# The opening of a Perceiver layer: loads on two queues in order of use, half of the tokens prepared after the first energies

## The chip, the cores and the metric

The kernel runs on one core of a Trainium2 chip. The metric is the device time of one launch in microseconds (us), lower is better. Engines are named as in the profile: PE (TensorE, with PEld for its weight loads), DVE (VectorE), ACT (ScalarE), POOL (GpSimd) and SP (SyncE, which in this kernel only issues DMAs). A trailing q, as in SPq, is an engine's instruction queue.

## The reference

One layer of a Perceiver on x (32 batches of 32 tokens, 256 wide) and a context of 257 rows per batch, cut to its steps:

```python
h = layernorm(x)                       # 1024 tokens
Q = h @ Wq.T + bq                      # 16 heads of 16
K, V = ctx @ Wk.T + bk, ctx @ Wv.T + bv
e = where(mask == 0, -1e20, Q K^T / 4); x = x + softmax(e) V @ Wo.T + bo
x = x + causal_self_attention_with_rope(layernorm(x))
x = x + top2_mixture_of_8_experts(layernorm(x))   # gelu(x w0) * (x w1) @ wo
```

All products of float32 data are made of three TensorE products of rounded halves: a value is split into a high part (an ACT copy that rounds) and a low part (DVE: value minus high part), and hi*lo + lo*hi + hi*hi is accumulated (`product3`). So each weight or activation that enters such a product costs a transpose on PE, an ACT copy and a DVE subtraction.

## The kernel before

The program has three stages: an opening ("prelude") that loads x and three weights and makes all queries; 32 steps of cross attention, one per batch b, arranged as 8 groups j of 4 (u = 0 to 3), into which the self attention of earlier groups is woven; and routing and expert products. Each engine has its own hand-written list of instructions; semaphores (`wait_ge`) are the only order between engines.

The prelude is a list `slots`: `bias` (biases turned), `w` 0 to 2 (Wq, Wk, Wv turned and split), `lastT` (the last context row of each batch), `kl` and `vl` (its key and value), `xT` 0 to 3 (256 normed tokens each, turned and split), `q` 0 to 3 (queries: two halves of the features, two halves of the tokens). PE works through it in that order, ACT keeps the high part, and DVE the low part. All of it has to be over (`first_act` and `first_dve` at their full counts) before `turn_ctx(0)` begins the cross attention: context 0 turned, `keys(0)`, `values(0)`, context 1 turned, and then step 0 with `energies(0)`.

In a step b the engines do, in this order: PE `energies(b)`, `turn_ctx(b+2)`, `keys(b+1)`, `outputs(b-2)`, `turn_probs(b-1)`, `values(b+1)`; ACT four exponentials with the split of context b+2 among them, then `keep_keys(b+1)` and `keep_values(b+1)`; DVE the four `maxima`, and so on; POOL spreads the queries (`spread`) and scales the probabilities. In group 0 five more weights are turned, at the end of each step (`late_weights`: weights 3 and 4 in step 0, 5 and 6 in step 1, 7 in step 2).

All loads are issued by SP, in one list. Weights in `BY_HEAD` (0, 1, 4, 5: Wq, Wk and the self attention's W_Q, W_K) are loaded with their rows rearranged, in two DMAs each of 128 KB. The zero fills of `V`, `PTd` and `Vm` are the first work of DVE; POOL adds the bias bo to x (`xbo_done`) before step 0.

```python
pe.wait_ge(sm["first_act"], NS)          # after all 15 slots
pe.wait_ge(sm["first_dve"], sum(by_dve))
turn_ctx(0, 0, 16); keys(0, 0); values(0, 0); turn_ctx(1, 1, 16)
```

## Time and profile before

| | |
|---|---|
| time, median of 3 runs | 563.48 us (563.48, 567.03, 556.87) |
| the profiled execution | 566.69 us, span 564.8 us |
| busy, share of the span | PE 501.6 us (89%), DVE 406.2 (72%), ACT 325.1 (58%), POOL 247.3 (44%) |
| PE busy from 0 to 10 us | none |
| PE busy from 10 to 20 us | 3.34 us |
| DMA | 48.91 MB, mean 87 GB/s |

The span runs from the first to the last instruction; 1.9 us of the profiled execution lie around it. Times in the trace count from the span's start. A matmul is pipelined, so its cost in a row of them is the distance between two starts, not its own duration. PEclk is the granted clock of TensorE, where 1.00 is 2.4 GHz and 0.50 is 1.2 GHz.

### The profile page before, as it was taken

The numbers are of one execution on the slowest core, as the hardware profiler recorded it, in microseconds if no ns is written. First come the engines' busy times: TensorE is split into PE (matmuls) and PEld (weight loads), VectorE is DVE, ScalarE is ACT, GpSimd is POOL, SyncE is SP. The second block draws the span as 40 slices with busy tenths as digits, with TensorE's granted clock in tenths as the row PEclk, the third lists the DMA queues.
The fourth block names the chain that finished last, engine by engine and source line by source line (L and its number), as shares of the span: only waits on it lengthen the run. The fifth ranks groups of instructions, "written<-read, shape, count | busy, mean of one in ns | idle before, by whom it ended". The sixth has DMA issues, their size and how long they took to land.

```text
span 564.8 us, 18262 instructions
## 1 busy us (share of the span) xinstructions
PE 501.6 (89%) x6637; PEld 460.1 (81%) x6637; DVE 406.2 (72%) x1005; ACT 325.1 (58%) x839; POOL 247.3 (44%) x337
## 2 busy tenths in 40 slices
PE   0777999989999999999976657899999999999996
PEld 0656778878889898888865546799999999999995
DVE  6414346477666767676676788599999999999973
ACT  0325667577667757676752215666665766657650
POOL 1301153344445364444430120366667667676650
PEclk9989899999999999999996765599999999999998
DMA  7420111121111111120006200055655656465302
GB/s 217 129 94 19 38 43 40 27 55 22 42 39 35 26 33 38 21 54 2 4 2 200 102 0 1 5 196 167 188 158 189 198 174 195 146 187 188 113 1 74
DMA packets 57981, 48.91 MB, mean 87 GB/s; under 512 B 20926, under 2 KB 49600, under 8 KB 57920
## 3 DMA queue, kind: packets, MB, share of 16 engines
q1 hardware_dynamic: 57920, 48.09, 28.9%
q8 instruction: 39, 0.64, 0.5%
q14 instruction: 22, 0.18, 0.1%
HBM read 46.86 MB, written 1.08 MB: 85 GB/s over the span
## 4 chain that ended last, share of the span: by engine, by line
PE 77%; ACT 7%; DVE 5%; issue 5%; DMA 2%; SPq 2%; POOL 0%; DVEq 0%; ACTq 0%; POOLq 0%
PE bank L215 20%; PE bank L217 18%; PE bank L216 18%; PE bank L556 5%; PE bank L534 3%; PE bank L580 3%; ACT Pr L994 2%; PE bank L491 2%; PE bank L925 2%; PE bank L711 1%; ACT PTd L1087 1%; DMA bias_raw<-in_L_xattn_bv 1%; PE bank L673 1%; DMA last_prob<-Pr 1%; PE bank L684 1%
## 5 line engine op out<-in xcount | busy, mean ns | idle before, releaser
L215 PE MATMUL bank<-XT_lo,W_hi 128*128 128x256 f32 (+1 forms) x352 | 100.5, 286 | 1.3 <-ACT CT L1166 1.3
L216 PE MATMUL bank<-XT_hi,W_lo 128*128 128x256 f32 (+1 forms) x352 | 100.1, 284 | 0.0
L217 PE MATMUL bank<-XT_hi,W_hi 128*128 128x256 f32 (+1 forms) x352 | 99.8, 284 | 0.0
L1876 POOL TENSOR_TENSOR W_lo<-raw,W_hi 128x256 fp32r<-128x256 f32 (+1 forms) x88 | 88.4, 1005 | 7.0
L1799 POOL TENSOR_TENSOR Pr<-Pr,rinv 128x1028 f32<-128x1028 f32 x31 | 58.9, 1901 | 51.1 <-DVE rinv L1307 50.4
L994 ACT ACTIVATE Pr<-Sc,nmax 128x257 f32<-128x257 f32 x128 | 63.8, 502 | 23.1 <-DVE nmax L1296 21.6
L1296 DVE CUSTOM_DVE_ANT_0 Sc<-bank,mask_add 128x257 f32<-128x257 f32 x128 | 46.9, 422 | 38.8 <-PE bank L534 16.8
L1738 DVE TENSOR_TENSOR hid_lo<-hid,hid_hi 128x256 fp32r<-128x256 f32 (+1 forms) x88 | 73.1, 831 | 1.5 <-ACT hid_hi L1215 1.5
L1708 DVE TENSOR_TENSOR W_lo<-raw,W_hi 128x512 fp32r<-128x512 f32 (+1 forms) x88 | 68.8, 784 | 5.2 <-ACT W_hi L1139 1.4
L1874 POOL CAST W_hi<-raw 128x256 fp32r<-128x256 f32 (+1 forms) x88 | 39.1, 444 | 74.3 <-PE bank L217 36.9
L215 PEld LDWEIGHTS bank<-XT_lo,W_hi 128*128 128x128 f32 (+1 forms) x352 | 66.6, 189 | 1.6 <-issue 1.6
L216 PEld LDWEIGHTS bank<-XT_hi,W_lo 128*128 128x128 f32 (+1 forms) x352 | 66.4, 189 | 0.0
L217 PEld LDWEIGHTS bank<-XT_hi,W_hi 128*128 128x128 f32 (+1 forms) x352 | 66.3, 188 | 0.0
L1211 ACT ACTIVATE act<-bank 128x256 f32<-128x256 f32 (+1 forms) x88 | 33.7, 383 | 53.9 <-PE bank L217 53.3
L1139 ACT ACTIVATE W_hi<-raw 128x512 fp32r<-128x512 f32 (+1 forms) x88 | 53.6, 612 | 0.0
L215 PE MATMUL bank<-W_lo,hid_hi 128*128 128x256 f32 (+1 forms) x176 | 49.7, 282 | 0.5 <-issue 0.5
L216 PE MATMUL bank<-W_hi,hid_lo 128*128 128x256 f32 (+1 forms) x176 | 49.5, 281 | 0.0
L217 PE MATMUL bank<-W_hi,hid_hi 128*128 128x256 f32 (+1 forms) x176 | 49.5, 281 | 0.0
L1215 ACT ACTIVATE hid_hi<-hid 128x256 fp32r<-128x256 f32 (+1 forms) x88 | 36.9, 419 | 14.2 <-DVE hid L1733 12.3
L1733 DVE TENSOR_TENSOR hid<-bank,act 128x256 f32<-128x256 f32 (+1 forms) x88 | 36.4, 414 | 11.8 <-ACT act L1211 11.5
L215 PE MATMUL bank<-WT_lo,ctxT_hi 128*128 128x256 f32 x128 | 40.1, 314 | 4.7 <-ACT KT L971 4.5
L215 PE MATMUL bank<-ctxT_lo,WT_hi 128*128 128x256 f32 x128 | 39.4, 308 | 1.5 <-DVE ctxT_lo L1281 1.5
(234 smaller groups left out, 1333.4 us busy)
## 6 DMA issues: line engine op xcount, KB each, us to landing
raw<-in_L_ffn_w_kernel SPq DMA_DIRECT2D x32, 512.0 KB, 4.6
ctx_raw<-in_ctx SPq DMA_DIRECT2D x32, 256.0 KB, 2.8
raw<-in_L_ffn_wo_kernel SPq DMA_DIRECT2D x16, 512.0 KB, 5.8
...
last_prob<-Pr SPq DMA_DIRECT2D x128, 1.0 KB, 1.8
...
```

Of the source, the lines that this page charges most:

```text
L215: pe.matmul(dst, a_hi, b_lo, start=first, stop=False)
L216: pe.matmul(dst, a_lo, b_hi, start=False, stop=False)
L217: return pe.matmul(dst, a_hi, b_hi, start=False, stop=last)
L994: ac.activation(Pr[:, r % 2, g, 0:SC], Sc[:, r % 2, g, 0:SC], ACT.Exp, bias=nmax[:, r % 2, g:g + 1], scale=-1.0, accum_out=Pr[:, r % 2, g, ...
L1139: ac.activation(W01_hi[:, (NT * half_ + n) % RW, :, :, 0:w].rearrange("p i k n -> p (i k) n"), raw01[:, :, :, t * P:t * P + w].rearrange(" ...
L1215: ac.activation(hid_hi[0:w, m % RW, :], hid[0:w, m % RH, :], ACT.Copy).then_inc(sm["hhi_done"], 1)
L1296: ve.tensor_tensor_reduce(Sc[:, r % 2, g, 0:SC], bk[g][:, 0:SC], mask_add[:, :], -0.25, 3e38, ALU.add, ALU.min, nmax[:, r % 2, g:g + 1]).t ...
L1708: ve.tensor_tensor(W01_lo[:, (NT * half_ + n) % RW, :, :, 0:w].rearrange("p i k n -> p (i k) n"), raw01[:, :, :, t * P:t * P + w].rearrang ...
L1738: ve.tensor_tensor(hid_lo[0:w, m % RW, :], hid[0:w, m % RH, :], f(hid_hi[0:w, m % RW, :]), ALU.subtract)\
L1799: po.tensor_tensor(Pr[:, r % 2, :, 0:SC], Pr[:, r % 2, :, 0:SC], rinv[:, r % 2, :].unsqueeze(2).broadcast_to([P, G, SC]), ALU.mult).then_i ...
L1874: po.tensor_copy(W2_hi[0:w, m % RW, :], raw2[0:w, t, :]).then_inc(sm["hi2"], 1)
L1876: po.tensor_tensor(W2_lo[0:w, m % RW, :], raw2[0:w, t, :], f(W2_hi[0:w, m % RW, :]), ALU.subtract)\
```

## The change

Loads. ACT now issues Wq, Wk and Wv as its first instructions. SP loads the identity columns of the constant table alone, then x tiles 0 to 3, the biases, context 0, the last rows, the rest of the table, context 1, the mask, x tiles 4 to 7, contexts 2 and 3, bo and the five other weights.

Prelude. Only the first half of the tokens is normed, turned and projected. The slots are now w 0, w 1, bias, lastT, xT 0, xT 1, w 2, q 0, q 1, kl, vl; `turn_ctx(0)`, `keys(0)` and `turn_ctx(1)` stand among them, and `values(0)` comes after `energies(0)`. The slots use six banks (0 to 3, 6, 7).

Moved behind. The second half's statistics and norms (`statistics(1)`, `norm_tokens(1)`) stand late in DVE's prelude; its turning (`late(0)`, `late(1)`) is in step 3 and its queries (`late(2)`, `late(3)`) in step 4. On PE and ACT the late weights now come ahead of `values(b+1)`/`keep_values(b+1)`, before behind them. The fills run on POOL, and its bias sums go into steps 0 to 3, two tiles each. `vl`, `xn` and the turned tokens get places of their own, in arrays that are used later.

```diff
-    slots = [("bias", 0)] + [("w", i) for i in range(WF)] + [("lastT", 0), ("kl", 0), ("vl", 0)]
-    slots += [("xT", c) for c in range(4)] + [("q", c) for c in range(4)]
+    slots = [("w", 0), ("w", 1), ("bias", 0), ("lastT", 0), ("xT", 0), ("xT", 1), ("w", 2), ("q", 0), ("q", 1), ("kl", 0), ("vl", 0)]
...
+    ROOM = (0, 1, 2, 3, 6, 7)
...
+        return {(0, 3, 0): (0,), (0, 3, 1): (1,), (1, 0, 0): (2,), (1, 0, 1): (3,)}.get((j, u, part), ()) if isinstance(j, int) else ()
...
-        sp.dma_start(tab[:, :], table).then_inc(sm["const_in"], 16)
+        sp.dma_start(tab[:, 0:P], table[:, 0:P]).then_inc(sm["const_in"], 16)
...
+        load_x(0)
+        load_x(1)
...
-        load_ctx(0, True)
-        sp.dma_start(bo_row[:, :], xbo.rearrange("(a n) -> a n", a=1).broadcast_to([P, D])).then_inc(sm["bo_in"], 16)
+        first_ctx(0)
+        sp.dma_start(last_raw[:, :], ctx_in[:, SC - 1, :]).then_inc(sm["last_in"], 16)
+        sp.dma_start(tab[:, P:NC_], table[:, P:NC_]).then_inc(sm["table_in"], 16)
+        first_ctx(1)
         for h in range(HG):
             sp.dma_start(mask_i[h * S:(h + 1) * S, :], mask[0, 0]).then_inc(sm["mask_in"], 16)
+        load_x(2)
+        load_x(3)
+        first_ctx(2)
+        first_ctx(3)
+        sp.dma_start(bo_row[:, :], xbo.rearrange("(a n) -> a n", a=1).broadcast_to([P, D])).then_inc(sm["bo_in"], 16)
         for i in range(WF, 8):
-            load_weight(i)
...
+        def late(n):
+
+            pe.wait_ge(sm["w_lo"], 8 - WF)
+            if n < 2:
+                pe.wait_ge(sm["lx_lo"], n)
+                turn_tokens(2 + n, bk[6]).then_inc(sm["lx_made"], 1)
+            else:
+                pe.wait_ge(sm["lx_hi"], 2)
+                pe.wait_ge(sm["lx_lo"], 2)
+                pe.wait_ge(sm["lq_kept"], n - 2)
+                queries(1, n - 2, bk[6]).then_inc(sm["lq_made"], 1)
 
...
+        for n in range(2):
+            prepare(n)
         turn_ctx(0, 0, 16)
+        for n in range(2, slot("w", 2) + 1):
+            prepare(n)
         keys(0, 0)
-        values(0, 0)
+        for n in range(slot("q", 0), slot("vl", 0)):
+            prepare(n)
         turn_ctx(1, 1, 16)
+        prepare(slot("vl", 0))
+        pe.wait_ge(sm["first_act"], NS)
+        pe.wait_ge(sm["first_dve"], sum(by_dve))
 
         def step(j):
 
             for u in range(4):
                 b = 4 * j + u
                 energies(b, u)
+                if isinstance(j, int) and b == 0:
+                    values(0, 0)
                 if u == 0:
...
-                values(b + 1, (u + 1) % 4)
                 for i in late_weights(j, u):
                     turn_weight(i)
+                for n in late_tokens(j, u, 1):
+                    late(n)
+                values(b + 1, (u + 1) % 4)
...
+        for i in range(WF):
+            load_weight(ac, i)
...
+        statistics(0)
+        low(slot("w", 0))
+        low(slot("w", 1))
+        norm_tokens(0)
         split_ctx(0, 0)
+        low(slot("lastT", 0))
+        low(slot("xT", 0))
+        low(slot("xT", 1))
+        low(slot("w", 2))
+        statistics(1)
+        set_mask()
         split_ctx(1, 1)
+        norm_tokens(1)
         ve.wait_ge(sm["maskb_set"], 1)
...
+        po.memset(V[:, :, :, :, :], 0.0).then_inc(sm["v_zero"], 1)
         po.wait_ge(sm["ones_set"], 1)
-        po.wait_ge(sm["ln1_var"], 1)
-        po.tensor_tensor(rstd[:, :], mv[:, :, 1], half[:, :], ALU.pow).then_inc(sm["ln1_rstd"], 1)
-        po.wait_ge(sm["const_in"], 16)
-        po.wait_ge(sm["bo_in"], 16)
-        po.wait_ge(sm["ln1_done"], TT)
-        for j in range(TT):
-            po.tensor_tensor(x_sb[:, j, :], x_sb[:, j, :], bo_row[:, :], ALU.add).then_inc(sm["xbo_done"], 1)
-        po.wait_ge(sm["first_act"], NS)
-        po.wait_ge(sm["first_dve"], sum(by_dve))
+        for part in range(2):
+            tiles = slice(TT // 2 * part, TT // 2 * (part + 1))
+            po.wait_ge(sm["ln1_var"], part + 1)
+            po.tensor_tensor(rstd[:, tiles], mv[:, tiles, 1], half[:, tiles], ALU.pow).then_inc(sm["ln1_rstd"], 1)
+            if part == 0:
+                po.memset(PTd[:, :, :, :, :], 0.0)
+                po.memset(Vm[:, :, :, :], 0.0).then_inc(sm["diag_zero"], 1)
+        po.wait_ge(sm["table_in"], 16)
+        po.wait_ge(sm["first_act"], slot("kl", 0) + 1)
+
+        def add_bias(u):
+
+            po.wait_ge(sm["bo_in"], 16)
+            po.wait_ge(sm["ln1_done"], TT)
+            for j in (2 * u, 2 * u + 1):
+                po.tensor_tensor(x_sb[:, j, :], x_sb[:, j, :], bo_row[:, :], ALU.add).then_inc(sm["xbo_done"], 1)
 
...
+                if isinstance(j, int) and j == 0:
+                    add_bias(u)
+                elif isinstance(j, int) and j == 1 and u == 0:
+                    po.wait_ge(sm["xbo_done"], TT)
+                    po.wait_ge(sm["lq_kept"], 2)
```

DVE's opening, as a listing of its instructions in program order. Before (`bn` and `mv` are statistics, `xn` the normed tokens, a name with `_lo` a low part):

```order
L1228 MEMSET V 128x3072
L1229 MEMSET PTd 128x2048
L1230 MEMSET Vm 128x1536
L1250 BN_STATS bn<-x_sb 128x6 x8
L1253 BN_AGGR mv<-bn 128x2 x8
L1255 TENSOR_SCALAR mv<-mv 128x8
L1245 TENSOR_TENSOR WT_lo<-bank,WT_hi 128x512 x3
L1245 TENSOR_TENSOR lastT_lo<-bank,lastT_hi 128x64
L1261 TENSOR_SCALAR xn<-x_sb,mv,rstd 128x256 x8
L1245 TENSOR_TENSOR xnT_lo<-bank,xnT_hi 128x2x256 x4
L1268 TENSOR_SCALAR mask_add<-mask_i 128x257
L1281 TENSOR_TENSOR ctxT_lo<-bank,ctxT_hi 128x512 x2
```

And now, from the place where the fills stood:

```order
L1338 BN_STATS bn<-x_sb 128x6 x4
L1341 BN_AGGR mv<-bn 128x2 x4
L1344 TENSOR_SCALAR mv<-mv 128x4
L1330 TENSOR_TENSOR WT_lo<-bank,WT_hi 128x512 x2
L1351 TENSOR_SCALAR xn<-x_sb,mv,rstd 128x256 x4
L1378 TENSOR_TENSOR ctxT_lo<-bank,ctxT_hi 128x512
L1330 TENSOR_TENSOR lastT_lo<-bank,lastT_hi 128x64
L1330 TENSOR_TENSOR xnT_lo<-bank,xnT_hi 128x2x256 x2
L1330 TENSOR_TENSOR WT_lo<-bank,WT_hi 128x512
L1338 BN_STATS bn<-x_sb 128x6 x4
L1341 BN_AGGR mv<-bn 128x2 x4
L1344 TENSOR_SCALAR mv<-mv 128x4
```

The first norms stand behind the low parts of two weights, no longer of three, and the second four tiles come at the end. The mask, the second context and the other four norms follow these rows.

The loads. Before, SP from its first load:

```order
L341 DMA tab<-in_table 128x682
L344 DMA x_sb<-in_x 128x2x256 x4
L337 DMA w_raw<-in_L_xattn_Wq 128x1x256 x2
L337 DMA w_raw<-in_L_xattn_Wk 128x1x256 x2
L339 DMA w_raw<-in_L_xattn_Wv 128x2x256
L347 DMA last_raw<-in_ctx 32x256
L354 DMA bias_raw<-in_L_xattn_bq 2x4x32
L354 DMA bias_raw<-in_L_xattn_bk 2x4x32
L354 DMA bias_raw<-in_L_xattn_bv 2x128
L365 DMA ctx_raw<-in_ctx 128x2x256 x4
```

Now SP, with the three weights gone to ACT:

```order
L359 DMA tab<-in_table 128x128
L363 DMA x_sb<-in_x 128x2x256 x2
L373 DMA bias_raw<-in_L_xattn_bq 2x4x32
L373 DMA bias_raw<-in_L_xattn_bk 2x4x32
L373 DMA bias_raw<-in_L_xattn_bv 2x128
L377 DMA ctx_raw<-in_ctx 128x2x256
L397 DMA last_raw<-in_ctx 32x256
L398 DMA tab<-in_table 128x554
L377 DMA ctx_raw<-in_ctx 128x2x256
L401 DMA mask_i<-in_mask_1x1xSxS_ik 32x257 x4
L363 DMA x_sb<-in_x 128x2x256 x2
```

What moved: the first weight is the first load of a queue, and nothing of x beyond four tiles stands ahead of context 0.

ACT in step 0 (Pr are the exponentials, KT and V the kept keys and values of batch 1, WT_hi the late weights). Before:

```order
L994 ACTIVATE Pr<-Sc,nmax 128x257
L962 ACTIVATE ctxT_hi<-bank 128x512
L994 ACTIVATE Pr<-Sc,nmax 128x257 x3
L971 ACTIVATE KT<-bank,bias_col 128x256 x2
L984 ACTIVATE V<-bank 128x16x2x16
L954 ACTIVATE WT_hi<-bank 128x512 x2
```

Now, with the values of batch 0 ahead of the first exponential:

```order
L1049 ACTIVATE V<-bank 128x16x2x16
L1059 ACTIVATE Pr<-Sc,nmax 128x257
L1027 ACTIVATE ctxT_hi<-bank 128x512
L1059 ACTIVATE Pr<-Sc,nmax 128x257 x3
L1036 ACTIVATE KT<-bank,bias_col 128x256 x2
L1019 ACTIVATE WT_hi<-bank 128x512 x2
L1049 ACTIVATE V<-bank 128x16x2x16
```

The late weights' high parts now precede the values of batch 1.

## Rows read from the trace of the kernel before

**Rows 1.** The page's first line.

```profile
span 564.8 us, 18262 instructions
```

**Rows 2.** The chain of work that ended last, 0 to 60 us: start, us, what.

```profile
8.81 6.53 DMA bias_raw<-in_L_xattn_bv
15.48 0.24 PE bank L435
15.72 2.77 PE bank L440 x12
...
20.47 0.21 PE bank L216
...
29.52 0.23 PE bank L216
...
35.66 0.67 PE bank L491 x4
...
38.21 0.21 PE bank L216
```

**Rows 3.** Busy time by stretch: us, engines, PEclk, DMA share, GB/s.

```profile
1.00:2.00 1.00, 0.00 (x0) 0.00 (x0) 0.41 (x4) 1.00 (x1) 0.00 (x0) 1.00 0.29 44
...
5.00:6.00 1.00, 0.00 (x0) 0.00 (x0) 1.00 (x1) 0.00 (x0) 0.00 (x0) 1.00 1.04 346
...
17.00:18.00 1.00, 1.00 (x6) 1.00 (x6) 0.57 (x1) 0.74 (x2) 0.00 (x0) 1.00 0.27 88
...
39.00:40.00 1.00, 1.00 (x7) 1.00 (x6) 0.00 (x0) 0.00 (x0) 0.00 (x0) 0.50 0.30 100
...
41.00:42.00 1.00, 0.51 (x2) 0.51 (x3) 0.00 (x0) 0.43 (x2) 0.00 (x0) 0.50 0.00 0
```

**Rows 4.** Timeline of the prelude: start, us, engine, line, operation, count, idle before.

```profile
1.63 2.62 DVE L1228 MEMSET V<- 128x3072 f32 x1 [0.59 <-issue]
3.20 1.36 SPq L337 DMA_DIRECT2D w_raw<-in_L_xattn_Wq  x2
...
16.80 0.60 ACT L937 ACTIVATE WT_hi<-bank 128x512 fp32r<-128x512 f32 x1 [0.87 <-PE bank L440]
17.43 0.69 DVE L1245 TENSOR_TENSOR WT_lo<-bank,WT_hi 128x512 fp32r<-128x512 f32 x1 [5.99 <-ACT WT_hi L937]
...
19.88 2.66 DVE L1261 TENSOR_SCALAR xn<-x_sb,mv,rstd 128x256 f32<-128x256 f32 x8
...
22.71 5.52 POOL L1761 TENSOR_TENSOR x_sb<-x_sb,bo_row 128x256 f32<-128x256 f32 x8 [9.46 <-DVE xn L1261]
...
27.15 6.69 SPq L387 DMA_DIRECT2D VL_all<-vl_rows  x8
```

**Rows 5.** Timeline of step 0 and the start of step 1.

```profile
45.05 0.69 PE L534 MATMUL bank<-KT,Qb 32*64 32x257 f32 x16
...
50.19 0.39 PE L215 MATMUL bank<-WT_lo,ctxT_hi 128*128 128x256 f32 x1 [1.52 <-ACT KT L971]
...
51.72 1.04 PE L592 MATMUL bank<-tab,w_raw 128*128 128x128 f32 x8
```

**Rows 6.** DVE's timeline, the first row of each later step's maxima, with what precedes it.

```profile
53.04 1.29 DVE L1272 TENSOR_TENSOR WT_lo<-bank,WT_hi 128x512 fp32r<-128x512 f32 x2 [4.37 <-ACT WT_hi L954]
54.24 0.17 DVE L1307 RECIPROCAL rinv<-Pr 128x4 f32<-128x4 f32 x1
54.33 0.40 DVE L1296 CUSTOM_DVE_ANT_0 Sc<-bank,mask_add 128x257 f32<-128x257 f32 x1
...
63.61 0.40 DVE L1296 CUSTOM_DVE_ANT_0 Sc<-bank,mask_add 128x257 f32<-128x257 f32 x1
...
70.93 0.40 DVE L1296 CUSTOM_DVE_ANT_0 Sc<-bank,mask_add 128x257 f32<-128x257 f32 x1
```

**Rows 7.** ACT's timeline: the values kept in steps 3 and 4.

```profile
76.74 0.60 ACT L984 ACTIVATE V<-bank 128x512 f32<-128x512 f32 x1 [1.30 <-PE bank L217]
...
83.15 0.60 ACT L984 ACTIVATE V<-bank 128x512 f32<-128x512 f32 x1 [1.31 <-PE bank L217]
```

**Rows 8.** Busy time by stretch, routing and experts (columns as in rows 3).

```profile
335.00:340.00 5.00, 3.05 (x14) 2.96 (x15) 4.72 (x15) 0.00 (x0) 1.71 (x3) 0.50 0.00 0
...
380.00:400.00 20.00, 20.00 (x171) 20.00 (x170) 19.28 (x31) 13.53 (x31) 12.95 (x19) 1.00 0.54 174
```

226 lines of the change are left out of this document (136 added, 90 removed).

## The prediction

> **What bounds the kernel now.** I read the page first, then the chain of waits over the first 60 us, then the timeline, then busy time by stretch. The span is 564.8 us [rows 1]; the profiled execution took 566.69 us, 1.9 us more, and the median of the three runs shown is 563.48, 3.2 us less. The chain shows that until 15.48 us PE has had nothing: it waits for the biases' load, issued at 8.81 and landed 6.53 us later behind all of x and three weights [rows 2]. From there to the first energies at 45.05 [rows 5] the chain is the prelude list itself, run in series: 29.6 us of turning, splitting and projecting. So the opening costs 45 us before the cross attention's cycle turns, and that cycle (one batch in 83.15 - 76.74 = 6.41 us [rows 7]) doesn't overlap it. Every us taken from the opening ends the kernel one us earlier, unless the steps behind it give it back.
>
> **When the loads land now.** The stretch from 5 to 6 us moved 346 GB/s at a DMA share of 1.05; the one from 17 to 18 us moved 88 GB/s at a share of 0.27 [rows 3]. What was in flight at 17 us were the `BY_HEAD` weights of the self attention, so a load of that form runs at about 90 GB/s, on a quarter of the DMA engines, and everything spread over all engines waits behind it on that quarter. Wq and Wk are 512 KB of that form: 5.7 us alone. The Trainium skill (DMA: Bandwidth & Descriptors, "Why a DMA increments its semaphore by 16 and not by 1") states that the number of engines divides the slowest dimension of both sides; this source's slowest dimension is 4, which gives 4 of 16, and the share of 0.27 agrees.
>
> Data begins to flow between 1 and 2 us [rows 3]; I take 2.0. If ACT's queue had the quarter to itself, Wk would land at 2.0 + 5.7 = 7.7 us. If the two queues take turns, SP's loads take half of it: its list up to x tile 7 is about 2 MB (64 KB table, 512 KB x, 256 KB context, 32 KB last rows, 277 KB table, 256 KB context, 128 KB mask, 512 KB x), a quarter of which, about 510 KB, passes there while Wk's last byte waits. Then 1.02 MB at 90 GB/s take 11.3 us and Wk lands at 13.3. I take 13.3, since both queues issue from the start. Wv and context 0 are there by about 15 us. Issuing costs ACT five DMAs at 0.34 to 0.7 us (1.36 us for two [rows 4]), about 3 us, at a time when it waits anyway.
>
> By the Trainium skill (DMA: Bandwidth & Descriptors, "Issuing engines are not separate DMA queues") a second issuing engine saves issue time only, because all DMAs end on the same 16 engines. By that rule the gain at the loads comes from the order alone; the sum below holds both ends, 7.7 and 13.3.
>
> **From Wk to the first energies.** PE runs its list in order, so I count from Wk's landing T.
> - Turning Wk: 4 of the 12 transposes that took 2.77 us [rows 2], 0.92. ACT's high part 0.60 and DVE's low part 0.69, with 0.3 of hops [rows 4]: T + 2.5.
> - DVE's norms stand behind that low part: 2 of 8 in 2.66 us [rows 4], 0.7: T + 3.2. Context 0, biases and last rows are turned meanwhile.
> - x tiles: 8 transposes at 0.23: T + 5.1. Wv: 0.92: T + 6.0.
> - `keys(0)`: 12 matmuls at 0.21 [rows 2]: T + 8.5. The context's low part needs a DVE operation behind four norms, T + 4.6, so it is in time.
> - `q` 0 and 1: 12 at 0.23 [rows 2]: T + 11.3. `kl` waits for ACT to keep the last query, 1.0 more; then 12 at 0.21: T + 14.9.
> - Context 1 (0.67 [rows 2]), `vl` 6 at 0.21, ACT's copy 0.6: T + 17.2. POOL spreads the queries meanwhile.
>
> With 13.3 this is 30.5 us, and by the faster spacing 20.00/171 = 0.117 us per 256 columns [rows 8] in `keys`, `kl` and `vl` it would be 2.8 us less. The distance 0.21 is 256 columns at 1.2 GHz, the granted level 0.50 that the row at 39 us shows, and 0.117 goes with level 1.00. I take 29.5: energies(0) 15.5 us earlier than 45.05.
>
> **What the steps give and take.**
> - `values(0)` and its copy now stand between energies(0) and the first exponential: 12 matmuls at 0.117 to 0.21 and 0.60 on ACT, 2.0 to 3.1 us, of which DVE's maxima hide about one. Cost 2.0 (1 to 2.5).
> - The late weights move ahead of `values(b+1)`. Before, PE turned them after the values (1.04 us at 51.72 [rows 5]), and DVE's low parts, 1.29 us, stood ahead of the reciprocal and the next maxima, which started at 54.33 [rows 6]. Now PE does them in the 1.52 us in which it waited for the keys [rows 5], and ACT while PE makes the values. The maxima of steps 1, 2, 3 are 9.28 and 7.32 us apart [rows 6], against a cycle of 6.41 [rows 7]: an excess of 2.9 and 0.9 us, and about 1.7 in step 0. I take 4.5 of these 5.5 as won; the low bound is 2, PE's transposes alone.
> - Late tokens. Eight transposes and 12 matmuls of 512 columns come into steps 3 and 4: PE 1.3 + 2.8 us, ACT two copies of 0.6 and two of 0.7, DVE 1.4. ACT's copies before `keep_keys` are in the cycle: 0.6 and 0.7. In step 4 PE's other work up to the values (about 3.9 us) plus 2.8 exceeds the 4.9 us it has, by 1.8. Sum 3.1; bounds 1.5 (PE's slack takes the queries) and 6.9 (PE 4.1 and ACT 2.8 in full).
> - Fills on POOL: 6656 columns, on DVE 2.62 us for 3072 [rows 4]. No row shows a fill of that size on POOL; its sum of 256 columns takes 5.52/8 = 0.69 us, which bounds 6656 columns at 18 us, and DVE's rate gives 5.7. The first norms need POOL after `V` alone: 2.6 to 8.3 us, before Wk's low part in either case. The rest ends by 26 at the latest, ahead of the first spread. Nothing. If that cover went, the excess would be paid in full at the norms.
> - Bias sums: 2 x 0.69 us per step on POOL, behind `normalise` and ahead of a spread needed a step later; POOL works 2.5 us of 6.4 in a step. Nothing.
> - DVE's second statistics and norms, 1.3 + 0.6 + 1.3 us, end at about T + 15.7 and so touch the first maxima by at most 0.7.
> - `VL_all` waits for `vl`, about 3 us later than before relative to the span's start; SP issues it for 6.69 us [rows 4], and the 0.30 share goes on until past 40 us and is over by 41 [rows 3]. So contexts 4 and 5, issued behind it, land near 45 us. Context 4 is needed in step 2, at 29.5 + 17 = 46.5. Just hidden; queued behind it are `keys(3)` and the whole cycle.
>
> **Sum.** 15.5 - 2.0 + 4.5 - 3.1 - 0.7 = 14.2 us. The profiled execution would be 552.5, the median 563.5 - 14.2 = 549.3. I say 549.
>
> **Rivals.**
> - A. ACT's queue isn't shared evenly and Wk lands at 8 to 10 us. For it: the loads of x are spread and the quarter is free after them. Against: SP issues faster than the quarter drains. PE then starts 4 us earlier, and the median is 545 or below. Chance 0.14.
> - B. The steps give more back. The late tokens cost 6.9, or context 4 comes 2 to 3 us late behind `VL_all`, and the weights win 2 rather than 4.5. Together 14.2 - 3.8 - 2.5 = 8 us: 555.5. For it: step 4 is full on PE and SP's queue is serial. Chance 0.26.
> - C. The loads gain nothing: the quarter of DMA engines is held by SP's list, 670 KB up to bo, before Wk, 15 us, and the extra hops eat the rest. Half of the tokens' work (1.8 + 2.8 us of PE) is then still out of the opening, and comes back in the steps: 563. Chance 0.05.
> - D. Slower: the clock. From 335 to 340 us the granted level is 0.50 with PE busy 3.05 of 5 us, and from 380 on it is 1.00 with PE busy 20 of 20 [rows 8]. All later work starts at other times, so the level could fall elsewhere. A us at 0.50 in the dense expert stage costs half a us. To be slower by over 2% this has to cost 14.2 + 11.3 = 25.5 us, so 51 us more at the low level than before. In the traces PE keeps 1.00 where it is dense. Chance 0.02. A tenth of it would shift the time by 2 or 3 us either way, and the three runs of before spread over 10 us.
>
> **How the numbers follow.** The forecast has 0.53, with its own range of 546 to 552.5: Wk between 11 and 15, the late tokens 1.5 to 4. A reaches down to 541 (T of 7.7 gives 5.6 us more, but then context and norms bound, and I keep 3.5, plus the spread of runs), B up to 557. The range is 541.5 to 557. A change of 2% is 11.3 us, about what a measurement of this kernel can tell from none: the line is 552.2. Faster: 0.14 of A, 0.50 of the forecast, 0.06 of B, so 0.70. Within 2%: the rest of the forecast and of B, and C: 0.28. Slower 0.02.
>
> **What would show it.** PE's first transpose near 8 us and Wk's near 13; the first norm right behind Wk's low part; energies(0) at 27 to 31; energies(1) 7 to 8 us behind; maxima of steps 1, 2, 3 6.5 us apart; steps 3 and 4 longer than 6.4 by 3 us in all; no wait for context 4. The forecast is wrong if Wk lands outside 10 to 15, if PE waits for a context in step 2, or if the stretch from 330 us on isn't the old one moved.

## The result and the profile after

| | before | after |
|---|---|---|
| median of 20 runs each | 565.84 us | 556.46 us (554.08 to 560.66) |
| ratio | | 0.9892, 95% interval 0.9872 to 0.9912 |
| span of the profiled execution | 564.8 us | 555.0 us |
| first kept values (ACT, `V`) | 44.45 | 36.45 |
| last kept values | 286.01 | 276.96 |

The changed kernel is faster by 1.1%, about 6 us; I had forecast 14. By the bound of 2% this is "no change that one can tell", to which I had given 0.28. The ratio leaves out disturbed runs, and with them the slower runs of before, so it lies nearer to 1 than the medians' 0.983. A second set of runs of the same two kernels gave 0.9831 (0.9783 to 0.9879), so "between 6 and 10 us" is what is known; the two profiled executions differ by 9.8.

The page's first line, against [rows 1]:

```profile
span 555.0 us, 18277 instructions
```

The chain of work that ended last, from the start to 60 us (start, us, what), against [rows 2]:

```profile
3.10 13.30 DMA w_raw<-in_L_xattn_Wk
16.44 1.13 PE bank L471 x4
...
19.61 1.97 PE bank L503 x8
...
32.39 1.16 PE bank L581 x16
...
36.95 0.59 ACT Pr L1059 x2
...
42.24 9.11 DMA ctx_raw<-in_ctx
51.40 0.66 PE bank L538 x4
```

Two loads now carry this chain: the keys' weights, which land at 16.40, and context 4, issued at 42.24 and on the way for 9.11 us. Before, the opening was bound by the biases' load and then by the list of work.

The timeline of the changed kernel around context 4. SP's queue is full with `VL_all`, the contexts come behind it, and behind these the small moves of the statistics (`last_prob`); PE and ACT then wait for both:

```profile
35.50 6.70 SPq L415 DMA_DIRECT2D VL_all<-vl_rows  x8
42.24 1.95 SPq L386 DMA_DIRECT2D ctx_raw<-in_ctx  x2
44.24 2.80 SPq L394 DMA_DIRECT2D last_prob<-Pr  x4
...
51.40 0.66 PE L538 MATMUL bank<-tab,ctx_raw 128*128 128x128 f32 x4 [2.37 <-DMA ctx_raw<-in_ctx]
...
53.01 0.51 ACT L1059 ACTIVATE Pr<-Sc,nmax 128x257 f32<-128x257 f32 x1 [3.96 <-DMA last_prob<-Pr]
```

ACT's timeline, the kept values of batches 0, 3, 4, 5 and 31; the last two of the first four answer to [rows 7]:

```profile
36.45 0.60 ACT L1049 ACTIVATE V<-bank 128x512 f32<-128x512 f32 x1 [4.11 <-PE bank L225]
...
58.56 0.60 ACT L1049 ACTIVATE V<-bank 128x512 f32<-128x512 f32 x1 [0.84 <-PE bank L225]
65.87 0.60 ACT L1049 ACTIVATE V<-bank 128x512 f32<-128x512 f32 x1 [0.84 <-PE bank L225]
74.42 0.60 ACT L1049 ACTIVATE V<-bank 128x512 f32<-128x512 f32 x1 [0.74 <-PE bank L225]
...
276.96 0.60 ACT L1049 ACTIVATE V<-bank 128x512 f32<-128x512 f32 x1 [1.30 <-PE bank L225]
```

These rows are the best ruler in this case, since every batch leaves one. The lead over before is 9.9 us at batch 1 (51.92 against 42.07), 12.3 at batch 2 (60.79 and 48.45), 10.6 at batch 3, 8.7 at batch 5, and 9.05 at batch 31. (Batch 0 compares badly, since its values now come behind the first energies.) So the opening earned 9.9, step 1 another 2.5, and steps 2 to 4 gave 3.6 back.

Busy time by stretch of the changed kernel (columns as in [rows 3]); the last two answer to [rows 8]:

```profile
2.00:4.00 2.00, 0.00 (x0) 0.00 (x0) 0.00 (x0) 0.00 (x0) 1.41 (x1) 1.00 0.71 208
4.00:6.00 2.00, 0.00 (x0) 0.00 (x0) 0.00 (x0) 1.28 (x1) 0.00 (x0) 1.00 0.64 158
...
330.00:355.00 25.00, 18.86 (x78) 16.67 (x79) 16.57 (x76) 15.47 (x32) 4.26 (x8) 0.50 0.00 1
380.00:400.00 20.00, 20.00 (x171) 20.00 (x170) 18.86 (x31) 12.76 (x30) 13.61 (x20) 1.00 0.59 181
```

The long stretch at level 0.50 in the routing is 34.1 us in both profiled executions (331.6 to 365.7 before, 321.7 to 355.9 after): the old one, moved by 9.8. In the first 62 us each of them has 10.2 us at level 0.50. The clock doesn't explain the shortfall.

### The profile page after: what moved, and what is told of

It is laid out like the page before. It is cut to its first block, busy times and chain, and to the rows that moved or that the text cites. A ratio compares the mean times of both kernels' runs of the same rounds, so it can differ in the third digit from the quotient of the medians.

```text
span 555.0 us, 18277 instructions
## 1 busy us (share of the span) xinstructions
PE 498.2 (90%) x6637; PEld 457.4 (82%) x6637; DVE 400.8 (72%) x1003; ACT 324.7 (59%) x839; POOL 252.6 (46%) x341
## 4 chain that ended last, share of the span: by engine, by line
PE 80%; ACT 5%; issue 5%; DVE 5%; DMA 4%; ACTq 1%; DVEq 0%
PE bank L223 20%; PE bank L225 18%; PE bank L224 18%; PE bank L603 5%; PE bank L627 3%; PE bank L581 3%; DMA w_raw<-in_L_xattn_Wk 2%; PE bank L538 2%; ACT Pr L1059 2%; DMA ctx_raw<-in_ctx 2%; PE bank L986 2%; PE bank L758 1%; ACT PTd L1152 1%; PE bank L720 1%; PE bank L731 1%
## 5 line engine op out<-in xcount | busy, mean ns | idle before, releaser
L1820 DVE TENSOR_TENSOR W_lo<-raw,W_hi 128x512 fp32r<-128x512 f32 (+1 forms) x88 | 70.3, 801 | 4.9 <-ACT W_hi L1226 1.4
L1850 DVE TENSOR_TENSOR hid_lo<-hid,hid_hi 128x256 fp32r<-128x256 f32 (+1 forms) x88 | 71.4, 811 | 1.5 <-ACT hid_hi L1302 1.5
L1298 ACT ACTIVATE act<-bank 128x256 f32<-128x256 f32 (+1 forms) x88 | 33.7, 383 | 52.7 <-PE bank L225 52.1
L1412 DVE COPY PT<-bank 128x512 f32<-128x512 f32 x32 | 22.1, 691 | 25.9 <-PE bank L603 25.7
```

Source lines behind the costliest of these rows:

```text
L1820: ve.tensor_tensor(W01_lo[:, (NT * half_ + n) % RW, :, :, 0:w].rearrange("p i k n -> p (i k) n"), raw01[:, :, :, t * P:t * P + w].rearrang ...
L1850: ve.tensor_tensor(hid_lo[0:w, m % RW, :], hid[0:w, m % RH, :], f(hid_hi[0:w, m % RW, :]), ALU.subtract)\
```

## Experiments

Three theories of where the expected gain went. **Loads**: Wq, Wk and `VL_all` each sit on a quarter of the DMA engines; that holds Wk until 16.4 us and context 4 and the last of the statistics' moves until 51 and 53. **Moved work**: what was moved into steps 2 to 4 costs more there. **Queue**: a second issuing engine brings nothing, or harm. All kernels are the changed one with one edit, unless said otherwise. The table gives the kept values' times in the profiled execution and the time against before, measured on the same chip.

| kernel | batch 0 | batch 3 | batch 5 | batch 31 | span | median | ratio to before (95%) |
|---|---|---|---|---|---|---|---|
| before | 44.45 | 69.12 | 83.15 | 286.01 | 564.8 | | |
| after | 36.45 | 58.56 | 74.42 | 276.96 | 555.0 | 556.46 | 0.9892 (.9872-.9912) |
| e0, after again | 35.45 | 55.31 | 71.20 | 274.95 | 553.7 | 555.59 | 0.9831 (.9783-.9879) |
| e1, contexts first | 35.32 | 53.75 | 69.62 | 273.11 | 553.9 | 555.44 | 0.9817 (.9779-.9855) |
| e2, weights spread | 28.95 | 48.90 | 64.78 | 268.08 | 548.4 | 550.34 | 0.9735 (.9695-.9774) |
| e3, `VL_all` spread | 35.57 | 54.15 | 70.04 | 273.55 | 550.2 | 554.96 | 0.9802 (.9770-.9835) |
| e4, e1 to e3 together | 29.09 | 47.63 | 63.51 | 267.03 | 547.9 | 548.55 | 0.9691 (.9624-.9758) |
| e5, weights behind | 36.67 | 58.63 | 75.42 | 278.80 | 559.6 | 559.94 | 0.9886 (.9813-.9958) |
| e6, tokens before | 47.37 | 65.86 | 78.69 | 282.20 | 561.8 | 562.91 | 0.9956 (.9920-.9991) |
| e7, one queue | 35.03 | 56.59 | 72.44 | 276.75 | 555.8 | 557.13 | 0.9849 (.9782-.9916) |
| e8, before with spread loads | 39.81 | 64.52 | 78.25 | 280.72 | 560.3 | 560.51 | 0.9923 (.9893-.9954) |
| e9, fills on DVE | 36.59 | 58.80 | 74.66 | 277.12 | 555.9 | 557.76 | 0.9896 (.9862-.9931) |
| e11, e4 again | 28.84 | 47.35 | 63.23 | 266.15 | 544.2 | 547.24 | 0.9711 (.9659-.9763) |
| e10, e4 and norms first | 26.26 | 44.62 | 60.49 | 263.24 | 541.4 | 547.57 | 0.9713 (.9665-.9761) |
| e15, e10 again | 29.22 | 47.58 | 63.43 | 266.76 | 546.8 | 548.22 | 0.9704 (.9658-.9750) |
| e12, e7 with fills held | 33.80 | 53.41 | 69.27 | 273.05 | 551.8 | 554.25 | 0.9823 (.9769-.9876) |
| e13, e10 with fills held | 28.14 | 46.49 | 62.35 | 265.72 | 545.7 | 545.59 | 0.9649 (.9604-.9693) |
| e14, e10 with fills early | 24.75 | 43.09 | 58.94 | 263.65 | 546.0 | 544.11 | 0.9626 (.9574-.9679) |

How far to trust it: behind batch 31 the code is the same in all of them (up to spread weights loaded long before), yet that part took 276.7 us (e3) to 282.4 (e14). Two us of a single span or of four runs' median say nothing; the kept values say more, but they too are those of one execution of each kernel.

### The changed kernel again (e0)

> The changed kernel itself, as the reference for the other kernels of this set. Expected 0.989 of the kernel before, about 556 us.

It ran 2 us faster at batch 31 than the profile first shown, and most of that is at step 2: batch 3 follows batch 2 after 7.9 us here, after 10.1 there. Context 4 landed at 48.60 here and at 51.36 there. SP's timeline of the first profile, then SP's and ACT's of e0:

```profile
32.36 0.33 SPq L411 DMA_DIRECT2D vl_rows<-vl  x1
```

```profile
31.36 0.33 SPq L411 DMA_DIRECT2D vl_rows<-vl  x1
32.85 6.62 SPq L415 DMA_DIRECT2D VL_all<-vl_rows  x8
39.52 2.12 SPq L386 DMA_DIRECT2D ctx_raw<-in_ctx  x2
...
50.24 0.51 ACT L1059 ACTIVATE Pr<-Sc,nmax 128x257 f32<-128x257 f32 x1 [2.24 <-DMA last_prob<-Pr]
```

Two things are to be read here. First, context 4 was on its way for as long in both (9.08 and 9.11 us from issue to landing); it was issued 2.7 us earlier. `VL_all` waits for the store of the last rows' values, and that store of 32 KB landed after 1.47 us here and after 3.12 there. In the kernels of the table it takes either 1.5 us (e0 to e3, e6, e8, e10 to e12, e14, e15) or 3.1 to 3.7 (the changed kernel, e4, e5, e7, e9, e13), with one of each for e4 and e11, which are the same kernel, and 2.57 in the kernel before; why, no run shows. Second, the wait that sets the step is not the one for context 4, which was 0.66 us here, but ACT's for the last of the four moves of the statistics, issued behind the contexts. In a clean step ACT idles 0.74 us at that place (e1, e3), for the maxima. What it idles beyond that is the step's excess over 6.41: 1.50 and 1.50 us in e0, 1.59 and 1.60 in e2, 1.16 and 1.16 in e12, 3.20 and 3.21 in e7. In the first profile it is 3.22 of 3.70. The other 0.5 goes with a stretch of 3.4 us at level 0.50 that begins at 52.1, when PE had been busy 0.60 us of the last 2; of the other kernels that have this wait only e9 has such a stretch there, and it too has 0.45 us more (2.80 of 3.25).

### The loads behind `VL_all` (e1, e3)

e1, on SP ahead of the store of the last rows' values:

```
+        for b in (4, 5):
+            sp.wait_ge(sm["ctx_turned"], b - 3)
+            src = ctx_in[b:b + 1, 0:2 * P, :].rearrange("a (t p) d -> p (a t) d", p=P)
+            sp.dma_start(ctx_raw[:, b % 4, :, :], src).then_inc(ctx_in_sem[b % 4], 16)
```

> The loads of contexts 4 and 5 are issued by SP as soon as their buffers are free, ahead of the store of the last rows' values and of the four loads that spread them over all tokens (VL_all); nothing else is changed. Theory 1 (step 2 of the changed kernel is long because context 4 is queued behind VL_all on the same DMA engines: it lands at 51.36, TensorE's copy of it waits 2.37 us, and the statistics' small move lands at 52.90, with ScalarE waiting 3.96 us): context 4 lands near 36, its wait at the context's transposes is gone, step 2 takes 6.4 to 7.5 us instead of 10.1, and the kernel is 2.5 to 3.7 us faster than the changed one. If only the small move of the statistics matters (it is still behind VL_all here), the wait of 3.96 us on ScalarE stays and the gain is under 1 us. Rival (the slow step is the work moved into it, not a load): no change, within 0.5 us.

e3, four DMAs of 32 destination rows in place of eight that each go to all 128 rows:

```
-        for j in range(TT):
-            src = vl_rows[BT * j:BT * j + BT, :].unsqueeze(1).broadcast_to([BT, S, D])
-            sp.dma_start(VL_all[:, j, :], src).then_inc(sm["vl_in"], 16)
+        by_batch = vl_rows.rearrange("(j b) n -> b j n", b=BT)
+        for q in range(BT):
+            sp.dma_start(VL_all[q * S:(q + 1) * S, :, :], by_batch[q].unsqueeze(0).broadcast_to([S, TT, D]))\
+              .then_inc(sm["vl_in"], 16)
```

> The four loads of VL_all go by 32 destination rows each with all batches' columns, over all DMA engines, in place of four loads that each go to all rows from a quarter of the engines; the contexts' loads stay behind them. Theory 1 (a quarter of the DMA engines is the place where context 4 and the statistics' move are late): VL_all lands 5 to 9 us before 50.62, context 4 at 44 to 46 and the statistics' move about 2 us after its issue, step 2 is 2.5 to 3.7 us shorter and the kernel as much faster. If the order alone matters and not the engines: VL_all lands as before and nothing changes. Rival (the slow step is the work moved into it): no change, within 0.5 us.

Timelines of SP, PE and ACT up to step 2, e1 and then e3:

```profile
32.72 6.65 SPq L421 DMA_DIRECT2D VL_all<-vl_rows  x8
...
47.85 0.66 PE L544 MATMUL bank<-tab,ctx_raw 128*128 128x128 f32 x4
...
53.75 0.60 ACT L1055 ACTIVATE V<-bank 128x512 f32<-128x512 f32 x1 [0.82 <-PE bank L225]
```

```profile
32.97 1.98 SPq L415 DMA_DIRECT2D VL_all<-vl_rows  x4
34.99 0.96 SPq L386 DMA_DIRECT2D ctx_raw<-in_ctx  x2
...
48.25 0.66 PE L539 MATMUL bank<-tab,ctx_raw 128*128 128x128 f32 x4
...
54.15 0.60 ACT L1050 ACTIVATE V<-bank 128x512 f32<-128x512 f32 x1 [0.82 <-PE bank L225]
```

Either edit removes both waits; PE's copy of context 4 has no idle time in front, ACT waits for no `last_prob`, and batch 3 follows batch 2 after 6.41 us, a clean step. With `VL_all` on all engines SP issues it in 1.98 us, it landed at 40.90 and context 4 at 41.39. So context 4 and the moves behind it were late for both reasons, order and engines, and the work moved into step 2 is not what made it long. The step gained 1.5 us against e0 and 3.7 against the first profile; of the total, e1's median shows nothing and e3's 0.6 us, within what the tail varies by. The mechanism is shown, its share in the total only by the kept values (1.8 us at batch 31 in e1, 1.4 in e3). One expectation missed: I said in e1 that ACT's wait for `last_prob` might stay, since these moves are still behind `VL_all`. The last of them landed at 47.49, in time: with the contexts no longer between them and `VL_all`, it took 2.3 us from issue to landing in place of 4.8 (e0).

### The weights' loads (e2)

```
+    SPREAD = (0, 1)
...
+        if i in SPREAD:
+            src = weights[i].rearrange("(r c x) n -> r x c n", r=HG, c=KH)
+            for r in range(HG):
+                eng.dma_start(w_raw[r * S:(r + 1) * S, i, :, :], src[r]).then_inc(w_in[i], 16)
```

> The weights of the queries and keys are loaded in four DMAs each, one for each 32 rows of the destination, in place of two each: the same bytes over all DMA engines in place of a quarter of them; nothing else is changed. Theory 1 (the keys' weights land at 16.39 us, 3.1 us later than forecast, because their two DMAs sit on a quarter of the engines, in turn with SP's loads): they land between 9 and 13 us, the first energies start 3 to 7 us before 32.39, and the kernel is 3 to 6 us faster than the changed one. Rival (the two queues together are at the limit of the memory's bytes, not of a few engines): the landing stays within 1 us of 16.4 and the time within 0.5 us. Second rival (the extra issues on ScalarE, four of about 1 us, and the tokens' loads that now share their engines with the weights, take it back): weights at 9 to 11 us, but tokens later by as much and the kernel within 1.5 us of the changed one.

PE's and ACT's timeline, and busy time by stretch, of e2:

```profile
8.91 1.11 PE L476 MATMUL bank<-tab,w_raw 128*128 128x128 f32 x4 [1.79 <-DMA w_raw<-in_L_xattn_Wk]
...
28.95 0.60 ACT L1054 ACTIVATE V<-bank 128x512 f32<-128x512 f32 x1 [3.80 <-PE bank L225]
```

```profile
2.00:4.00 2.00, 0.00 (x0) 0.00 (x0) 0.00 (x0) 0.00 (x0) 1.41 (x1) 1.00 0.95 276
4.00:6.00 2.00, 0.00 (x0) 0.00 (x0) 0.75 (x2) 0.83 (x1) 0.00 (x0) 1.00 1.08 297
```

Wk landed at 8.87 in place of 15.56 (e0), and the DMA engines are full from 2 us on, where the changed kernel left a third of them free (shares 0.71 and 0.64). The first kept values came 6.5 us earlier, the last 6.9, and the median is 5.3 us lower: of the edits to the loads the one whose gain stands clear of the noise, and it brings over half of what the whole change did. The second rival fell: ACT's eight issues took 3.9 us, the tokens landed at 4.29 and 6.07, earlier than before.

### The whole of e1 to e3 (e4, e11)

> Three load edits on the changed kernel at once: the weights 0, 1, 4 and 5 in four DMAs of 32 destination rows each, VL_all in four such DMAs, and contexts 4 and 5 issued ahead of it. If the two places (a quarter of the DMA engines for the keys' weights, worth 6.5 us at the first kept values in the run with spread weights; context 4 and the statistics' move behind VL_all, worth 1.6 to 3.7 us) are separate and add: the first kept values at 29 us, those of step 3 at 47.5 instead of 55.3, 546 to 549 us in all, 0.965 to 0.970 of the kernel before. If what comes after takes it back (a later stage that doesn't follow): 550 us as with the weights alone.

> The three load edits together, once more, as the neighbour of the kernel that has the norms' order as well: 0.969 of the kernel before, 547 to 549 us, with the first kept values at 29.1 and the tokens' transposes at 12.3 us.

By the kept values they add: batch 3 at 47.63 and 47.35, steps 1 and 2 clean. By the times, 0.9691 and 0.9711 against 0.9735 for the weights alone is not told apart.

### Undoing a part (e5, e6, e9)

e5 puts the late weights behind the values again (PE; ACT alike; DVE's list is as it was):

```
-                for i in late_weights(j, u):
-                    turn_weight(i)
                 for n in late_tokens(j, u, 1):
                     late(n)
                 values(b + 1, (u + 1) % 4)
+                for i in late_weights(j, u):
+                    turn_weight(i)
```

> Undoes one part of the change: in steps 0 and 1 (and where late weights follow) TensorE turns the late weights behind the next batch's values again, not ahead of them, and VectorE and ScalarE follow. The forecast's working put this part at 4.5 us (bound 2). Theory 1: the steps' spacing goes back to about 7.5 us for the first and 8.9 for the second (5.6 and 6.4 in the changed kernel), and the kernel is 3 to 4.5 us slower than the changed one, 559 to 560 us. Rival (the gain in the early steps is covered by the wait for context 4, which is late anyway): 0 to 1.5 us slower, since context 4's wait shrinks by what the steps before it lose.

ACT's timeline of e5, batches 1 to 3:

```profile
42.23 0.60 ACT L1049 ACTIVATE V<-bank 128x512 f32<-128x512 f32 x1 [1.79 <-PE bank L225]
...
50.15 0.60 ACT L1049 ACTIVATE V<-bank 128x512 f32<-128x512 f32 x1 [1.30 <-PE bank L225]
...
58.63 0.60 ACT L1049 ACTIVATE V<-bank 128x512 f32<-128x512 f32 x1 [1.31 <-PE bank L225]
```

The step from batch 1 to 2 takes 7.9 us in place of 6.4, the one from 3 to 4 8.2 in place of 7.3, and the one between them 8.5 in place of 7.9 (e0) or 10.1 (after). From batch 0 to 5 it is 38.75 us against 35.75 in e0 and 37.97 in the first profile. Only the second pair compares like with like: the store ahead of `VL_all` took 3.38 us here, 3.12 in the first profile and 1.47 in e0. So the steps before and behind step 2 lose 2.5 us, step 2 gives 1.6 of it back, and 0.8 is left (1.8 at batch 31). The 3.0 against e0 has the late store in it and is too much. Theory and rival were both partly right: step 2's wait takes back part of what the other steps win.

e6 calls `late(0)` to `late(3)` at the end of the prelude on PE and ACT, and the low parts on DVE there too:

```
-        return {(0, 3, 0): (0,), (0, 3, 1): (1,), (1, 0, 0): (2,), (1, 0, 1): (3,)}.get((j, u, part), ()) if isinstance(j, int) else ()
+        return ()
```

> Undoes one part of the change: the second half of the tokens is turned and its queries made before the first step again, with VectorE's norms, instead of inside steps 3 and 4. Nothing else is changed; the turned copies keep the changed kernel's places. Theory 1 (the step forecast at 3.1 us of cost inside steps 3 and 4, which the trace shows at 3.0, against some 10 us of TensorE and ScalarE work taken out of the way to the first kept values): first kept values at 42 to 46 us instead of 35.5, steps 3 and 4 shorter by 3, and the kernel 4 to 7 us slower, 560 to 563. Rival (most of that work would have stood in gaps that the loads leave, so moving it brought little): less than 2 us slower.

ACT's timeline of e6:

```profile
47.37 0.60 ACT L1051 ACTIVATE V<-bank 128x512 f32<-128x512 f32 x1 [2.42 <-PE bank L225]
```

Batch 0 comes 11.9 us later, more than the 42 to 46 expected allow, and batches 0 to 5 then take 31.32 us in place of 35.75 (3.0 of it for the late tokens, 1.4 for step 2's wait). The net is 7.3 us at batch 31 (282.20 and 274.95), and 0.6 to 1.3% by the ratios. The rival fell. But 7.3 is an upper figure for what moving the tokens is worth, since e6 does the work worse than a prelude has to: the four pieces share one bank, and PE waits for ACT or DVE ahead of each of them (0.8 to 1.5 us), and the level is 0.50 from 31.1 to 44.7 us, so its 12 matmuls of 512 columns stand 0.43 apart and not 0.23. Its first energies stand at 45.00, where they stood before (45.05 [rows 5]); that is no measure of what the redrawn loads bring.

e9 puts the three fills back on DVE.

> Undoes one part of the change: the fills of V and of the three diagonal tiles go back to VectorE, ahead of its first statistics (2.62 us for V in the kernel before); nothing else is changed. The forecast put this part at nothing. VectorE waits 3 us for the first tokens anyway and then 2 to 5 us for the keys' weights, so 0 to 0.5 us slower than the changed one. Rival (the statistics start later by the fills and the tokens' norms with them, which the reciprocal roots on GpSimd and the transposes at 19.6 us wait for): the transposes of the tokens and all behind them 1 to 3 us later.

No difference to the changed kernel (0.9896 and 0.9892; the tokens' transposes start at 19.76 and 19.61), as forecast.

### One queue, and the fills beside the norms (e7, e12)

e7: Wq and Wk issued by SP ahead of the tokens, Wv behind the last rows, none by ACT.

> The three weights are issued on SP's queue, those of queries and keys ahead of the tokens and the values' behind the last rows, and ScalarE issues none. Forms and bytes are as in the changed kernel. Theory 1 (the keys' weights are late because the second queue's two DMAs take turns on a quarter of the engines with SP's loads): they land at 8 to 10 us instead of 16.4 and the tokens at 10 to 12; the first energies start 2 to 5 us before 32.4 and the kernel is 2 to 4 us faster than the changed one. Rival (two queues are what brings the gain of the redrawn prelude, as the change has it): keys' weights or tokens at over 16 us, and the kernel 0 to 3 us slower.

The weights did come earlier, at 11.23 us (not at 8 to 10), and nothing came of it: batch 0 at 35.03, and a median 1.5 us above e0's, which the rival had allowed, though neither load came later than 16. One reason is the tokens, which landed at 12.60. The other stands in the timelines of DVE, POOL and PE:

```profile
15.20 4.14 DVE L1351 TENSOR_SCALAR xn<-x_sb,mv,rstd 128x256 f32<-128x256 f32 x4
...
15.11 1.80 POOL L1873 MEMSET PTd<- 128x2048 f32 x1
16.85 1.38 POOL L1874 MEMSET Vm<- 128x1536 f32 x1
...
18.74 1.97 PE L506 MATMUL bank<-tab,xn 128*128 128x128 f32 x8 [3.41 <-DVE xn L1351]
```

The four norms took 4.14 us; in the changed kernel, behind the fills and not beside them, they took 1.37. e12 holds the fills back with one wait on POOL:

```
             if part == 0:
+                po.wait_ge(sm["ln1_done"], TT // 2)
                 po.memset(PTd[:, :, :, :, :], 0.0)
```

> The one-queue kernel again (weights on SP's queue), and GpSimd holds its two fills of 3.2 us (PTd and Vm) back until VectorE has normed the first tokens. In the one-queue run the keys' weights landed 4.3 us earlier, yet the tokens' transposes started at 18.74 as before, behind four norms that took 4.14 us in place of 1.37, with the two fills at 15.11 to 18.2 beside them. If the fills beside them are the cause: the norms take 1.4 us, the transposes start at 16.0, the first kept values come at 32.3 instead of 35.0, and the time is 2 to 3 us shorter, about 554.5. Rival (the norms wait for something else, the tokens or the reciprocal roots): they stay at 4.1 us and nothing changes.

```profile
16.25 1.38 DVE L1351 TENSOR_SCALAR xn<-x_sb,mv,rstd 128x256 f32<-128x256 f32 x4
...
17.69 1.80 POOL L1874 MEMSET PTd<- 128x2048 f32 x1 [1.48 <-DVE xn L1351]
...
17.04 1.97 PE L506 MATMUL bank<-tab,xn 128*128 128x128 f32 x8 [1.01 <-DVE xn L1351]
```

Confirmed: 1.38 us. The tokens landed 1.05 us later in this execution, so batch 0 is 1.2 us earlier and not 2.7; counted from the tokens' landing it is 20.2 us in place of 22.4. The Trainium skill (GPSIMD Engine Reference, "Specifications") says that GpSimd shares interfaces to the on-chip memory with VectorE and collides with VectorE's instructions in a two-port mode or with two inputs from there; the norms are of the first sort by its VectorE page (VectorE: DVE Perf Modes, "The perf-mode tier table"), which lists `tensor_scalar` on float32 in on-chip memory at 2x and, as the two-port mode needs both read ports of that memory, at 1x once an operand is in PSUM. The trace agrees: 4.14 us beside the fills, 1.38 without. With the fills held, one queue ran at 0.9823, two queues at 0.9831 and 0.9892: the second queue brings nothing that can be measured.

### The load's form in the old kernel (e8)

> The kernel before, with the weights 0, 1, 4 and 5 and VL_all loaded in four DMAs of 32 destination rows each, as in the runs on the changed kernel; its order of loads, its single queue and its prelude are as they were. If the loads' form on a quarter of the DMA engines is a bound there too: weights land 5 to 7 us earlier, but its prelude starts with TensorE at 15.48 us behind the biases' load, so the first kept values come 4 to 7 us earlier and the kernel takes 558 to 561 us. Rival (the old prelude is bound by its order and by the number of norms and queries in it, and not by bytes): under 2 us gained.

The kernel before, with nothing but spread loads, gains 4.6 us at batch 0 and 0.8% in all (0.9923). The biases' load, behind the weights, then landed 4.6 us earlier (PE started at 10.88, not 15.48). The first theory held. The form of the loads alone brings 0.8% in the old kernel, where the whole change brings 1.1 to 1.7%.

### Towards a better kernel (e10, e15, e13, e14)

e10 and e15 norm the first tokens ahead of the low part of the keys' weights:

```
         low(slot("w", 0))
-        low(slot("w", 1))
         norm_tokens(0)
+        low(slot("w", 1))
```

> The three load edits together (weights 0, 1, 4, 5 and VL_all over all DMA engines, contexts 4 and 5 ahead of VL_all) and, on VectorE, the first tokens' norms ahead of the low part of the keys' weights. In the run with the three edits the tokens' transposes start at 12.27 us, 0.75 us after TensorE was free, since the norms stand behind the split of the keys' weights at 10.88. Expected: transposes at 11.4 to 11.5, the first kept values at 28.2 instead of 29.1, 0.8 us faster than the three edits alone, 546 to 548 us, about 0.968 of the kernel before. If the split of the keys' weights, which the keys wait for, is what sets the start of the products: no change.

> The best kernel so far once more, beside the two that move its fills: 0.971 of the kernel before, norms at 3.8 us.

> The best kernel so far (three load edits, norms ahead of the keys' weights' low part) with the two fills held back until the first tokens are normed. There the norms took 3.77 us at 8.48 to 12.25, beside the fills at 8.02 to 11.2, and put the low part of the keys' weights to 12.18. If the fills are the cause: norms 1.4 us, the low part at 10.9, and the products start 0 to 1 us earlier than with the fills beside them (TensorE is busy with the tokens' transposes until 13.6 and the values' weights until 14.3), so 0 to 1 us in the time, 546.5 to 547.5. If not: norms at 3.8 us.

> The same kernel with the two fills right behind the fill of V, from 3.4 to 6.6 us, ahead of the reciprocal roots. If a fill on GpSimd slows whatever VectorE does beside it, the first tokens' statistics (4.45 to 6.6, 1.4 us of work) stretch to 2 to 4 us and the norms move back by as much, 0 to 2 us slower than with the fills held. If it slows the norms alone (a scalar operation of two columns' operands, not the statistics): statistics at 0.37 us each as before, norms 1.4 us, and the same time as with the fills held.

The norms alone brought nothing that shows in the time (0.9713 and 0.9704 against 0.9711): they then met the fills and took 3.77 and 4.13 us. With the fills held (e13) or put at the start (e14) they take 1.37. In e14 the fills stood beside the statistics, and these took 0.75 us for two as ever: this operation isn't slowed. The medians are 2.6 and 4.1 us below e15's on the same chip, more than the 0 to 1 expected for e13, but the intervals overlap, and the tokens' transposes start only 1.0 us earlier (11.54 and 11.65 against 12.55). That the held fills take the norms back to 1.4 us is shown; what they are worth in the time is not. e14 has the lowest median of all, 0.9626 or 544.1 us against 564.0 on the same chip, its six runs between 540.9 and 547.8.

Between e13 and e14 batch 0 differs by 3.4 us, though the tokens' transposes start at 11.54 and 11.65. Most of it is the granted clock. Busy time by stretch, e13 and then e14:

```profile
18.00:20.00 2.00, 1.02 (x6) 0.55 (x4) 0.00 (x0) 1.00 (x2) 0.75 (x1) 1.00 0.60 162
22.00:24.00 2.00, 1.46 (x6) 0.86 (x6) 1.42 (x4) 0.89 (x2) 1.01 (x4) 0.50 0.47 120
26.00:28.00 2.00, 2.00 (x11) 2.00 (x11) 0.97 (x6) 0.00 (x0) 0.61 (x3) 0.50 0.01 1
```

```profile
18.00:20.00 2.00, 1.18 (x11) 1.21 (x11) 0.00 (x0) 0.57 (x1) 0.35 (x1) 1.00 0.69 188
22.00:24.00 2.00, 1.62 (x24) 1.23 (x25) 2.00 (x8) 0.33 (x1) 0.40 (x1) 1.00 0.44 138
26.00:28.00 2.00, 2.00 (x18) 1.78 (x16) 0.69 (x1) 2.00 (x8) 0.00 (x0) 1.00 1.01 250
```

e13 runs at level 0.50 from 22.0 to 28.8 us with PE busy nearly throughout; e14 has no such stretch. From the first matmul of `kl` to batch 0's kept values it is 8.22 us in e13 and 5.93 in e14, 2.3 of the 3.4. The other 1.1 had arisen before: the matmuls of `keys(0)` follow each other after 0.21 us in e13 until 15.2 and after 0.12 in e14 from 13.8 on, though PEclk reads 1.00 in both. All other kernels of the table have a stretch at 0.50 of 3.4 to 13.7 us in their opening. Two executions of one and the same kernel differ nearly as much: 3.4 us at 0.50 in e10, 6.8 in e15, and batch 0 at 26.26 and 29.22, of which the tokens' transposes (11.66 and 12.55) account for 0.9. So the 3.4 us can't be put down to e14's early fills; whether they have a part in it was not tried.

## Why the prediction was wrong

The mechanism was right, the size was not: 14.2 us forecast, 9.8 between the profiled executions. Step by step:

- **Wk lands at 13.3.** It landed at 16.40 (e0: 15.56), 3.1 us later. This step failed. I let Wk share its quarter with SP's list and counted 1.02 MB; at 90 GB/s the 14.4 us to 16.4 are 1.3 MB. I had left out ACT's own Wv, the contexts behind the second tokens, bo and Wo; a quarter of them is 0.29 MB, which makes up the 1.3. That is an estimate: all of them were issued before 16.4, and so was W_Q on the same quarter (12.66), but no view shows whose bytes went first (Wv landed at 17.70). The share of all DMA engines was 1.02 and more from 6 to 14 us. That the form of the load is the cause is shown by e2 (8.87 with the same bytes in four pieces), and that the order has a part in it by e7 (11.23 ahead of the tokens). The lower end of my sum, 7.7 with the quarter for itself, was reached in no run. The end I called C (15 us, chance 0.05) was nearer than my value.
- **From Wk to the first energies 16.2.** 32.39 - 16.40 = 16.0. Right, and again in e2 (25.20 - 8.87 = 16.3). The gain there was 12.7 in place of 15.5; the weights' landing is all of the difference. Two readings in it were not. I took the matmuls of `kl` at 0.21 apart, as at 20.47 of [rows 2]; they stand 0.11 apart now and took 1.3 us in place of 2.5, with PEclk 1.00 in both stretches. And I tied 0.21 for 256 columns to the granted level 0.50, but `keys(0)` ran at 0.21 from 22.4 to 24.8 us, where PEclk reads 1.00. So a 1.00 in that column doesn't say that matmuls stand as close as they can; what spaced them, no row shows.
- **values(0) costs 2.0.** The first exponential came 36.95 - 32.39 = 4.6 us behind the energies, against 1.8 before, so this part cost 2.8: the matmuls stood at 0.21, level 0.50. That is 0.8 too little, and just above my bounds of 1 to 2.5.
- **Late weights win 4.5.** The steps from batch 1 to 4 were 8.87, 8.33 and 7.62 us, 5.6 over three of 6.41. Step 1 is clean now (6.38), and of the other two's excess what is left has other causes (below), so up to 5.6 were won. e5 shows less: undoing the part on PE and ACT costs 2.5 us in the steps beside step 2, of which step 2's wait returns 1.6.
- **Context 4 just hidden.** Failed, and as rival B said. It was wanted at 49.0 and landed at 51.36. Behind it came the statistics' four moves, which I had not counted at all: the last landed at 52.90 and held ACT for 3.96 us, and by e0, e2, e7 and e12 that wait is what the step's excess consists of. Step 2 was 3.7 us too long (3.2 of this wait, 0.5 at level 0.50), 1.5 in e0. I counted the contexts in SP's queue and forgot the four small moves behind them.
- **Late tokens 3.1.** 3.0, in steps 3 and 4 (7.3 and 8.55 us against 6.4). Right.
- **Fills nothing, bias sums nothing.** Right in time (e9), but for the fills on a cover that I named too loosely. It is not only that they end before they are needed: they must not stand beside the norms. Wk's late landing kept them apart; where it came early, or the norms stood ahead of its low part, they took 2.4 to 2.8 us longer (e7, e10, e15). The two pages of the Trainium skill named above say that such operations collide, and I had not weighed it.
- **DVE's second norms 0.7.** They ended before the first maxima and cost nothing.
- **The clock, D.** Excluded for this pair by the stretches above. Between executions of one kernel it moves the opening by some 2 us (e10 and e15).

By these sizes the lead at batch 5 is 12.7 - 2.8 + 5.6 - 3.7 - 3.0 = 8.8, and the rows show 8.7; with step 2's wait as in e0 it would be 11.0, near that set's medians (10.2). The 5.6 in it is the whole excess of before; it is no measurement of the late weights alone. Against the forecast 2.8 are missing at Wk's landing, 0.8 at the values and 1.5 to 3.7 in step 2, and 1.1 at the weights and 0.7 at the norms came in addition. What happened is rival B's size by B's and C's mechanisms together, where I had kept them apart. And the 2% line lay inside my own range: a forecast of 0.53 to one case whose own range reached across the line made "faster 0.70" too bold.
